# A graph, mixing and expert layer on one core: edge comparisons in five rounds, and work moved between waits

## The chip, the core and the metric

The kernel runs on one of the eight cores of a Trainium2 chip. A core has five engines with a program each: PE (TensorE, matrix products into PSUM, eight banks), DVE (VectorE), ACT (ScalarE), POOL (GpSimd) and SP (SyncE, which only starts transfers). They wait for one another by semaphores. The metric is the device time of one launch in microseconds, lower is better. Shown are three runs of the kernel before: 1836.55 us in the median, 1814.46 the lowest, 1837.39 the highest.

## The reference

x is 3125 x 256 with 53125 directed edges, sorted by destination. With n the layer norm of x:

```python
x = x + gnn(n, edges, ...) + mix(n, ...)      # both read the same n
x = x + ffn(layernorm(x), ...)
# gnn, three layers, widths 1024, 512, 256:
deg = segment_sum(1, dst) + 1; dinv = deg ** -0.5
h = relu(A @ (h @ W) + b), layer norm;  A[d, s] = edges(s, d) * dinv[s] * dinv[d], plus dinv^2 on the diagonal
# mix, on hyperbolic maps of n:
qkv = relu(batchnorm(n' @ Wqkv)); t = norm limits; s = pointwise(t)
out = (v k^T q) / (sum(v) + eps), per head;  ft = out @ Wres + b
```

The batch norm needs mean and variance of 768 columns over all rows. Edges may repeat, so the matrix A needs the number of equal (source, destination) pairs.

## The kernel before

The first third (0 to 350 us) does two things on the same engines. One is the mixing branch: rows of x are normed and turned, the Gram matrix of all rows is summed on PE, and the variance of each of the 768 columns comes from it: the matrix is turned and weighed with the weights (`weigh_gram_halves`), multiplied with the weights on DVE (`gw`), and summed by one-column matmuls (`bnsum_done`). Then five column blocks c of 625 rows each go through `hidden(c, m)` (six products of 12 matmuls into two pairs of banks, evacuated and squared by ACT), `spread(c, m)` (six products with `wp`), `norm_pair`, `norm_spread`, and on DVE `key`, `quotients`, `weigh`. Block c + 1's products stand in the program beside block c's quotients.

The other is the edges. Equal edges lie at most 40 places apart in the sorted list, or a flag says that they don't. DVE compares the key of each of 104 x 512 edges with those 1 to 40 places on (`equality`, `alike`, the result f16), and PE adds the 40 comparisons forwards and backwards into banks 6 and 7 by products with the identity (`count_alike`, 80 matmuls of 512 columns). The sums become an index and a value for each edge; PE turns them (`turn_edges`), DVE and ACT copy them out (`eidx`, `evalue`, L1737), and POOL scatters them into the matrix of counts in memory: 26 groups of 16 indirect transfers (L722). After the sixteenth transfer of a group it waits for the group before and raises `landed` (`landing`, L712 to L716). SP fetches one tile of counts for each row tile of the first layer, four buffers ahead at most, and waits for as many groups as that tile needs (L560). Degrees are counted by PE from one-hots (`degree(b)`, 16 matmuls) which DVE makes (`half_batch(b)`, L903 and L905, three buffers); there are 26 batches, of which `EARLY` come before the second block's products.

ACT also sums squares of the later weights (`weight_squares`, L1671, 28 pieces): pieces 0 to 12 stood between the veps of block 0 and the products of block 1.

From 350 us on, three layers of the graph network and the expert layer are bound by PE; the change doesn't touch them. Every order here is written out by hand.

## Time and profile before

| | us |
|---|---|
| median of three runs | 1836.55 |
| lowest, highest | 1814.46, 1837.39 |
| span of the profiled execution | 1299.6 |
| PE, DVE, POOL, ACT busy | 1189.9, 734.1, 563.5, 477.4 |

The profiler took one execution; the page gives its span from the first to the last instruction, and no other time of it. What lies around the span (launch and end) is the difference to a run's time, 537 us against the median. PE is busy for 92% of the span, but its share is lower in the first third, and a busy PE may run at half clock, so the row PEclk is read with it. A row of the trace in order of time gives start, duration, engine, line, operation, what it writes and reads, how many were merged, and in brackets how long the engine was idle before it and what ended that.

### The profile page before, as it was taken

To read this page: it belongs to the slowest core of one execution; us is meant where nothing else is said; L and a number is where in the kernel's file an instruction comes from. 1 tells how busy PE (TensorE), PEld (TensorE's weight loads), DVE (VectorE), ACT (ScalarE), POOL (GpSimd) and SP (SyncE) were. 2 spreads that over 40 slices of the span, in tenths; PEclk is the share of its full clock that TensorE was granted. 3 is DMA by queue.
4 is the path that set the end of the run, shared out by engine and by line. 5 is a ranking of instruction groups with operands and counts; after the bars stand their busy time and mean duration, and the time that the engine had idled before them with its cause. 6 is when DMAs were issued, how large, how long until landed. Compare 5 with 4: busy or idle time off the path is not lost.

```text
span 1299.6 us, 19205 instructions
## 1 busy us (share of the span) xinstructions
PE 1189.9 (92%) x6591; PEld 785.5 (60%) x6591; DVE 734.1 (56%) x1559; ACT 477.4 (37%) x1003; POOL 563.5 (43%) x579
## 2 busy tenths in 40 slices
PE   2897798988889999999999999999999899995995
PEld 2664465565556666666666566666666566652674
DVE  7875889687645554555455423333323388887253
ACT  4528565688432222222222113111111144441463
POOL 4207787778776777777774000350000000000633
PEclk9979989999889999999999999999999999998998
DMA  9881000001432222212143333323323256623201
GB/s 265 282 285 54 1 2 1 2 1 26 123 87 63 57 61 81 56 28 56 28 98 83 115 79 97 89 73 97 88 72 96 66 163 186 167 69 119 52 18 34
DMA packets 82936, 111.25 MB, mean 86 GB/s; under 512 B 51871, under 2 KB 67348, under 8 KB 82872
## 3 DMA queue, kind: packets, MB, share of 16 engines
q1 hardware_dynamic: 62344, 106.98, 29.9%
q0 software_dynamic: 20528, 3.47, 1.9%
q8 instruction: 34, 0.56, 0.2%
q14 instruction: 30, 0.25, 0.1%
HBM read 76.08 MB, written 27.67 MB: 80 GB/s over the span
## 4 chain that ended last, share of the span: by engine, by line
PE 83%; DVE 9%; ACT 5%; issue 2%; DMA 0%; POOL 0%; SPq 0%; ACTq 0%; DVEq 0%; POOLq 0%
PE psum L2044 80%; PE psum L2415 2%; DVE acc L903 1%; ACT acc L1613 1%; DVE scr L923 1%; ACT scr L1671 1%; DVE scr L1163 1%; PE psum L2408 0%; DVE scr L1469 0%; ACT scr L1741 0%; ACT scr L1767 0%; DVE big L917 0%; ACT scr L1748 0%; DVE acc L905 0%; DMA scr<-in_src_pad 0%
## 5 line engine op out<-in xcount | busy, mean ns | idle before, releaser
L722 POOL DMA_INDIRECT counts<-big,eidx x416 | 439.0, 1055 | 160.9 <-issue 160.9
L2044 PE MATMUL psum<-rows,scr 125*125 125x512 f16 x1250 | 276.4, 381 | 3.6 <-DVE rows L1266 1.6
L2044 PE MATMUL psum<-big,scr 125*125 125x512 f16 x1250 | 274.6, 379 | 1.0 <-DVE big L1300 1.0
L2044 PEld LDWEIGHTS psum<-rows,scr 125*125 125x125 f16 x1250 | 171.2, 137 | 104.1 <-issue 4.5
L2044 PEld LDWEIGHTS psum<-big,scr 125*125 125x125 f16 x1250 | 169.9, 137 | 96.5 <-DVE big L1300 1.5
L2044 PE MATMUL psum<-wb,scr 128*125 128x512 f16 x600 | 137.5, 379 | 1.4 <-DVE scr L1283 1.4
L2044 PEld LDWEIGHTS psum<-wb,scr 128*125 128x125 f16 x600 | 81.0, 136 | 45.9 <-DVE scr L1283 1.9
L774 POOL DMA_INDIRECT scr<-picked,eidx x13 | 22.9, 1758 | 182.7 <-issue 182.7
L1358 DVE SCALAR_TENSOR_TENSOR scr<-psum,col,wm 125x512 f32<-125x512 f32 x25 | 18.8, 751 | 128.9 <-PE psum L2044 128.9
L2044 PE MATMUL psum<-big,wm 128*128 128x313 f16 (+1 forms) x432 | 75.6, 328 | 8.8 <-ACT scr L1728 7.3
L1283 DVE TENSOR_TENSOR scr<-psum,scr 128x1000 f16<-128x1000 f32 x25 | 30.0, 1200 | 86.5 <-ACT scr L1882 86.5
L1940 ACT ACTIVATE scr<-scr 125x512 f32<-125x512 f32 x25 | 15.7, 629 | 166.1 <-DVE scr L1358 166.1
L828 DVE BATCH_NORM_STATS2 col<-scr 125x6 f32<-125x512 f32 x75 | 49.6, 689 | 45.5 <-ACT scr L1891 28.1
L2044 PE MATMUL psum<-wa,scr 128*125 128x512 f16 x300 | 71.8, 391 | 0.9 <-DVE scr L1278 0.9
L763 POOL IOTA scr<- 125x63 f32 x1 | 0.2, 201 | 159.9 <-PE psum L2044 159.9
L2044 PEld LDWEIGHTS psum<-big,wm 128*128 128x128 f16 (+1 forms) x432 | 48.1, 115 | 34.8 <-ACT scr L1728 8.1
L2044 PEld LDWEIGHTS psum<-wa,scr 128*125 128x125 f16 x300 | 42.3, 141 | 26.2 <-issue 2.6
L754 POOL TENSOR_SCALAR scr<-wa,col 128x512 f32<-128x512 f32 x4 | 6.4, 1591 | 116.4 <-DVE col L1374 116.1
L1882 ACT CAST scr<-psum 128x1000 f16<-128x1000 f32 x25 | 24.8, 992 | 81.2 <-PE psum L2044 71.8
L2044 PE MATMUL psum<-wm,scr 128*125 128x256 f32 (+2 forms) x156 | 41.7, 413 | 0.0
L2044 PE MATMUL psum<-acc 128*32 128x125 bf16 (+2 forms) x516 | 29.5, 257 | 12.8 <-DVE acc L905 11.4
L1163 DVE RECIPROCAL scr<-scr 128x626 f32<-128x626 f32 x10 | 40.7, 4066 | 0.3
(421 smaller groups left out, 1840.9 us busy)
## 6 DMA issues: line engine op xcount, KB each, us to landing
scr<-counts SPq DMA_DIRECT2D x75, 683.6 KB
counts<-wb SPq DMA_DIRECT2D x25, 683.6 KB
counts<-big,eidx POOLq DMA_INDIRECT x416
scr<-counts SPq DMA_DIRECT2D x75, 79.3 KB
scr<-in_x SPq DMA_DIRECT2D x25, 125.0 KB
picked<-big SPq DMA_DIRECT2D x5, 566.6 KB
rows<-in_x SPq DMA_DIRECT2D x5, 560.0 KB
out<-acc SPq DMA_DIRECT2D x5, 560.0 KB
```

Of the source, the lines that this page charges most:

```text
L722: pool.indirect_dma_start(cells, bass.IndirectOffsetOnAxis(ap=eidx[:, r * EQ + g:r * EQ + g + 1], axis=0), evalue[:, at_c:at_c + 1], None, ...
L774: pool.indirect_dma_start(got[:, g, :], None, picked_dram, bass.IndirectOffsetOnAxis(ap=picked[:, g:g + 1], axis=0), bounds_check=N - 1, o ...
L828: done.did(dve.bn_stats(st2[:, h, :], src[:, h * 512:(h + 1) * 512] if parts > 1 else src))
L903: done.did(dve.tensor_tensor(ohp, free(edp16, b * DB, [[2, DB // 2], [0, P], [1, 2]]), free(iop, 0, [[0, DB // 2], [2, P], [1, 2]]), ALU.i ...
L923: dve.tensor_tensor(alike[r % 2][:, lo:hi, :], free(ekey, 0, [[0, hi - lo], [1, EQW]]), free(ekey, 1 + r * SHIFTS + lo, [[1, hi - lo], [1, ...
L1163: done.did(dve.reciprocal(tdiv, tdiv))
L1283: dve.tensor_tensor(xT16[:, 1].rearrange("p (b k) q -> p b (k q)", b=2), turned_halves(), xT16[:, 0].rearrange("p (b k) q -> p b (k q)", b ...
L1358: dve.scalar_tensor_tensor(out=pre[b][:, 0:D2], in0=bank(b, P, D2), scalar=d2out[:, bass.ds(t, 1)], in1=b2r, op0=ALU.mult, op1=ALU.add).th ...
L1882: act.copy(xT16[:, 0].rearrange("p (b k) q -> p b (k q)", b=2), turned_halves()).then_inc(sem("xThi_done"), 1)
L1940: act.activation(pre[b][:, 0:D2], pre[b][:, 0:D2], ACT.Relu).then_inc(sem("relu2_done"), 1)
L2044: return pe.matmul(o, l, r, start=start, stop=stop)
L2415: last = pe.transpose(bank(5 + k // 4, 128, P, k % 4 * P), pre[0][:, k * 128:(k + 1) * 128], ident[:P, 0:P])
```

## The change

Nothing is computed otherwise. The edge comparisons come in five rounds of 8, 4, 10, 10 and 8 shifts, each with a place of its own where the memory is free (one in the region that the first products fill later), in place of four rounds of 10 in halves. Two rounds stand before the batch norm, one in its wait, two after it; the flag work comes behind the batch norm, and the flag's row is added on PE before the last two rounds are counted. The counts stand between the first block's products. Indices are turned after all six products. The flag is read by DVE behind round five. Five batches of one-hots and three of degrees move into the spread of block 0. ACT's squares 0 to 12 move behind the kept norms of block 1. POOL reports a group after four transfers of the next.

```diff
@@ -40,7 +40,7 @@
 DB = 16
-EARLY = 2
+EARLY = 5
 DEGREE_RUNS = (15, 11)
@@ -49,8 +49,8 @@
 HUGE = 3e38
-SHIFTS = 10
-ROUNDS_EQ = HALO // SHIFTS
+EQUAL_ROUNDS = ((0, 8), (8, 12), (12, 22), (22, 32), (32, 40))
+assert EQUAL_ROUNDS[-1][1] == HALO
 EQW = EC + HALO
@@ -254,8 +254,11 @@
-    alike = [scr[:ER, s * SHIFTS * EQW // 2:(s + 1) * SHIFTS * EQW // 2].bitcast(F16).rearrange(
-        "p (s i) -> p s i", s=SHIFTS) for s in range(2)]
+    ahead = big[:ER, pairs_at + 2 * 768:pairs_at + NT * CW]
+    behind = scr[:ER, at_edges + 7 * EW + 2 * EC:at_edges + 2 * NT * CW]
+    homes = (ahead, behind, scr[:ER, 0:5 * EQW], scr[:ER, 5 * EQW:10 * EQW], behind)
+    alike = [free(home.bitcast(F16), 0, [[EQW, hi - lo], [1, EQW]]) for home, (lo, hi) in zip(homes, EQUAL_ROUNDS)]
+    assert all((hi - lo) * EQW <= 2 * home.shape[1] for home, (lo, hi) in zip(homes, EQUAL_ROUNDS))
@@ -468,7 +471,7 @@
-    HALF_BATCHES = (((2, 2), (2, 2), (2, 5), (5, 8), (8, 12), (12, 15)),
+    HALF_BATCHES = (((5, 5), (5, 5), (5, 7), (7, 10), (10, 13), (13, 15)),
                     ((15, 16), (16, 16), (16, 18), (18, 22), (22, 24), (24, 26)))
@@ -722,8 +725,8 @@
                                             oob_is_err=False).then_inc(sem(f"scattered{n % 2}"), 16)
-            if n >= 1:
-                landing(n - 1)
+                if n >= 1 and r == n * ROWS_A_GROUP:
+                    landing(n - 1)
         landing(GROUPS - 1)
@@ -917,23 +920,21 @@
-        def equality(r, lo=0, hi=SHIFTS):
-            if r >= 2:
-                dve.wait_ge(sem("alike_used"), r - 1)
-            dve.tensor_tensor(alike[r % 2][:, lo:hi, :], free(ekey, 0, [[0, hi - lo], [1, EQW]]),
-                              free(ekey, 1 + r * SHIFTS + lo, [[1, hi - lo], [1, EQW]]), ALU.is_equal).then_inc(
-                sem("alike_ready"), hi - lo)
+        def equality(r):
+            lo, hi = EQUAL_ROUNDS[r]
+            if r == 4:
+                dve.wait_ge(sem("alike_used"), 2)
+            dve.tensor_tensor(alike[r], free(ekey, 0, [[0, hi - lo], [1, EQW]]),
+                              free(ekey, 1 + lo, [[1, hi - lo], [1, EQW]]), ALU.is_equal).then_inc(sem("alike_ready"), 1)
         done.settle()
         z_low(0)
         z_low(1)
-        equality(0, 0, 5)
+        equality(0)
         z_low(2)
-        equality(0, 5, 10)
         z_low(3)
-        equality(1, 0, 5)
         z_low(4)
-        equality(1, 5, 10)
+        equality(1)
         dve.wait_ge(milestone("zrow_done"), AFTER["zrow_done"])
@@ -959,6 +960,21 @@
                                      op0=ALU.mult, op1=ALU.subtract).then_inc(sem("wq_low"), 1)
+        dve.wait_ge(milestone("bnsum_done"), AFTER["bnsum_done"])
+        dve.tensor_scalar(tmp6, bank(3, 128, NT), 1.0 / N, None, ALU.mult).then_inc(milestone("bnvar_done"), 1)
+        done.did(dve.tensor_scalar(bnt, bank(3, 128, NT, 16), 1.0 / N, None, ALU.mult))
+        done.settle()
+        dve.wait_ge(milestone("bnroot_done"), AFTER["bnroot_done"])
...
+        dve.tensor_tensor(bnt, bnb, bnt, ALU.subtract).then_inc(milestone("bn_done"), 1)
+
         dstf = wkey
@@ -973,26 +989,12 @@
         done.did(dve.tensor_tensor(self_, free(dstf, HALO, [[1, EC]]), self_, ALU.is_equal))
-        dve.wait_ge(milestone("bnsum_done"), AFTER["bnsum_done"])
-        dve.tensor_scalar(tmp6, bank(3, 128, NT), 1.0 / N, None, ALU.mult).then_inc(milestone("bnvar_done"), 1)
-        done.did(dve.tensor_scalar(bnt, bank(3, 128, NT, 16), 1.0 / N, None, ALU.mult))
-        done.settle()
-        dve.wait_ge(milestone("bnroot_done"), AFTER["bnroot_done"])
...
-        dve.tensor_tensor(bnt, bnb, bnt, ALU.subtract).then_inc(milestone("bn_done"), 1)
-
         equality(3)
         dve.wait_ge(milestone("flag_part"), AFTER["flag_part"])
...
         done.settle()
+        equality(4)
         dve.wait_ge(milestone("flag_sum"), AFTER["flag_sum"])
@@ -1022,13 +1024,12 @@
-        dve.wait_ge(sem("alike_used"), ROUNDS_EQ)
+        dve.wait_ge(sem("alike_used"), len(EQUAL_ROUNDS))
         done.did(dve.tensor_tensor(bwd, bank(7, ER, EC), bwd, ALU.add))
-        done.did(dve.tensor_tensor(fwd, bank(6, ER, EC), fwd, ALU.add))
-        done.settle()
-
+        done.settle()
         done.did(dve.scalar_tensor_tensor(out=bwd, in0=bwd, scalar=2.0e7, in1=free(ekey, HALO, [[1, EC]]),
                                           op0=ALU.mult, op1=ALU.add))
+        done.did(dve.tensor_tensor(fwd, bank(6, ER, EC), fwd, ALU.add))
         done.settle()
@@ -1056,6 +1057,8 @@
         dve.tensor_scalar(needs[0:1, :], bank(6, 1, T, 128), 1.0, None, ALU.max).then_inc(milestone("needs_ready"), 1)
+        for b in range(2, EARLY):
+            half_batch(b)
         done.settle()
@@ -1732,9 +1735,6 @@
             hidden(0, m)
-            if m == 2:
-                act.wait_ge(milestone("value_turned"), AFTER["value_turned"])
-                act.copy(evalue, bank(7, 128, EQ * ER)).then_inc(milestone("value_kept"), 1)
@@ -1778,6 +1778,8 @@
+        act.wait_ge(milestone("value_turned"), AFTER["value_turned"])
+        act.copy(evalue, bank(7, 128, EQ * ER)).then_inc(milestone("value_kept"), 1)
         for m in range(NT):
@@ -1803,12 +1805,12 @@
                 rows_high(0, 4)
-            if c < 2:
+            if c == 1:
                 weight_squares(*SQUARES_AT[c][0])
             if c >= 1:
                 out_root(c - 1)
             besides(c, 0)
-            if c < 2:
+            if c == 1:
                 weight_squares(*SQUARES_AT[c][1])
@@ -1822,9 +1824,13 @@
             norm_keep(c + 1)
+            if c == 0:
+                weight_squares(*SQUARES_AT[c][0])
             veps_made(c + 1)
             out_square(c, 2)
             out_square(c, 3)
+            if c == 0:
+                weight_squares(*SQUARES_AT[c][1])
             besides(c, 3)
@@ -2047,14 +2053,16 @@
-        def count_alike(r, lo=0, hi=SHIFTS):
-            pe.wait_ge(sem("alike_ready"), r * SHIFTS + hi)
+        def count_alike(r, lo=0, hi=None):
+            first_shift, end = EQUAL_ROUNDS[r]
+            hi = end - first_shift if hi is None else hi
+            pe.wait_ge(sem("alike_ready"), r + 1)
             for k in range(lo, hi):
-                first, final = r + k == 0, r * SHIFTS + k == HALO - 1
-                behind = HALO - 1 - r * SHIFTS - k
-                mm(bank(6, ER, EC), ident16[:ER, 0:ER], alike[r % 2][:, k, HALO:HALO + EC], first, final)
-                last = mm(bank(7, ER, EC), ident16[:ER, 0:ER], alike[r % 2][:, k, behind:behind + EC], first, final)
-            if hi == SHIFTS:
+                shift = first_shift + k
+                after = HALO - 1 - shift
+                mm(bank(6, ER, EC), ident16[:ER, 0:ER], alike[r][:, k, HALO:HALO + EC], shift == 0, after == 0)
+                last = mm(bank(7, ER, EC), ident16[:ER, 0:ER], alike[r][:, k, after:after + EC], shift == 0, after == 0)
+            if hi == end - first_shift:
                 last.then_inc(sem("alike_used"), 1)
@@ -2126,7 +2134,7 @@
         last.then_inc(milestone("wq_summed"), 1)
-        count_alike(0, 3, SHIFTS)
+        count_alike(0, 3, 6)
@@ -2148,15 +2156,12 @@
         last.then_inc(milestone("wq_read"), 1)
-        count_alike(1, 0, 5)
+        count_alike(0, 6)
         pe.wait_ge(sem("wgw_done"), 1)
         for m in range(NT):
             last = mm(bank(3, 128, 1, m), gw[:, 0, m * 128:(m + 1) * 128], ones[:, 0:1], True, True)
         last.then_inc(milestone("bnsum_done"), 1)
-        count_alike(1, 5, SHIFTS)
-        pe.wait_ge(milestone("flag_part"), AFTER["flag_part"])
-        mm(bank(5, 1, 1, 400), ones[:ER, 0:1], flagf[:ER], True, True).then_inc(milestone("flag_sum"), 1)
-        count_alike(2)
+        count_alike(1)
@@ -2300,17 +2305,30 @@
-        for m in range(NT):
-            hidden(0, m)
-            if m == 0:
-                count_alike(3)
-            if m == 2:
-                turn_edges("index", 6, bwd)
-                turn_edges("value", 7, fwd)
+        hidden(0, 0)
+        count_alike(2, 0, 5)
+        hidden(0, 1)
+        count_alike(2, 5)
+        hidden(0, 2)
+        pe.wait_ge(milestone("flag_part"), AFTER["flag_part"])
+        mm(bank(5, 1, 1, 400), ones[:ER, 0:1], flagf[:ER], True, True).then_inc(milestone("flag_sum"), 1)
+        count_alike(3, 0, 5)
+        hidden(0, 3)
+        count_alike(3, 5)
+        count_alike(4)
+        hidden(0, 4)
+        hidden(0, 5)
+        turn_edges("index", 6, bwd)
+        turn_edges("value", 7, fwd)
+        spread(0, 0, 2)
         turn_reach()
-        spread(0, 0, 2)
+        spread(0, 2, 3)
         turn_needed()
-        spread(0, 2, NT)
+        degree(0)
+        spread(0, 3, 4)
+        degree(1)
+        spread(0, 4, NT)
+        degree(2)
         norm_pair(0, 5)
@@ -2324,7 +2342,7 @@
             if c == 0:
-                for b in range(EARLY):
+                for b in range(3, EARLY):
                     degree(b)
```

The milestones' names are put in the new order, and an assertion on sizes changes with them. The batch norm rows cut above are the same ones.

On PE, from the last counts before the Gram matrix is turned (`ident,scr 128x128`) up to the first product (`big,wm 128x313`, the next row before, and shown now); `scr,ident 104x512` and `big,ident 104x512` are counts. Before:

```order
L2044 MATMUL psum<-scr,ident 104x512 x14
L2134 MATMUL psum<-ident,scr 128x128
L2044 MATMUL psum<-wm,scr 128x512 x2
L2044 MATMUL psum<-wm,scr 128x256 x2
L2044 MATMUL psum<-wm,scr 128x512 x2
L2044 MATMUL psum<-wm,scr 128x256 x2
L2044 MATMUL psum<-col,wm 128x1 x12
L2044 MATMUL psum<-scr,ident 104x512 x10
L2044 MATMUL psum<-ones,big 128x1 x6
L2044 MATMUL psum<-scr,ident 104x512 x10
L2044 MATMUL psum<-col,ones 1x1
L2044 MATMUL psum<-scr,ident 104x512 x20
```

Now:

```order
L2050 MATMUL psum<-big,ident 104x512 x6
L2142 MATMUL psum<-ident,scr 128x128
L2050 MATMUL psum<-wm,scr 128x512 x2
L2050 MATMUL psum<-wm,scr 128x256 x2
L2050 MATMUL psum<-wm,scr 128x512 x2
L2050 MATMUL psum<-wm,scr 128x256 x2
L2050 MATMUL psum<-col,wm 128x1 x12
L2050 MATMUL psum<-big,ident 104x512 x4
L2050 MATMUL psum<-ones,big 128x1 x6
L2050 MATMUL psum<-scr,ident 104x512 x8
L2050 MATMUL psum<-big,wm 128x313 x12
L2050 MATMUL psum<-scr,ident 104x512 x10
```

Fewer counts stand before the turn and before the one-column products of the variance, and the first product comes after 12 + 12 of the 80 counts, not after 60.

On DVE, in the turning of the rows (L917, now L920, copies a turned block; L923, now L927, is `equality`) up to the correction of the Gram matrix (`col,psum 128x256`). Before:

```order
L923 TENSOR_TENSOR scr<-scr 104x2760
L917 SCALAR_TENSOR_TENSOR big<-psum,big 128x500 x2
L917 SCALAR_TENSOR_TENSOR big<-psum,big 128x2x125
L923 TENSOR_TENSOR scr<-scr 104x2760
L917 SCALAR_TENSOR_TENSOR big<-psum,big 128x500 x2
L917 SCALAR_TENSOR_TENSOR big<-psum,big 128x2x125
L923 TENSOR_TENSOR scr<-scr 104x2760
L917 SCALAR_TENSOR_TENSOR big<-psum,big 128x500 x2
L917 SCALAR_TENSOR_TENSOR big<-psum,big 128x2x125
L923 TENSOR_TENSOR scr<-scr 104x2760
L938 SCALAR_TENSOR_TENSOR scr<-big,col,psum 128x256
L940 SCALAR_TENSOR_TENSOR scr<-big,col,psum 128x128
```

Now:

```order
L927 TENSOR_TENSOR big<-scr 104x4416
L920 SCALAR_TENSOR_TENSOR big<-psum,big 128x500 x2
L920 SCALAR_TENSOR_TENSOR big<-psum,big 128x2x125
L920 SCALAR_TENSOR_TENSOR big<-psum,big 128x500 x2
L920 SCALAR_TENSOR_TENSOR big<-psum,big 128x2x125
L920 SCALAR_TENSOR_TENSOR big<-psum,big 128x500 x2
L920 SCALAR_TENSOR_TENSOR big<-psum,big 128x2x125
L927 TENSOR_TENSOR scr<-scr 104x2208
L939 SCALAR_TENSOR_TENSOR scr<-big,col,psum 128x256
L941 SCALAR_TENSOR_TENSOR scr<-big,col,psum 128x128
```

Four comparisons of five shifts have become one of eight and one of four.

On ACT, behind the kept norms (`acc<-psum 128x313`) of block 0 before, and of block 1 now; 1774 to 1778 is the veps root. Before:

```order
L1752 COPY acc<-psum 128x313
L1774 ACTIVATE scr<-psum,col 128x626
L1777 ACTIVATE scr<-scr,col 128x626
L1778 ACTIVATE acc<-psum,col 1x626
L1671 ACTIVATE scr,col<-wa 128x512 x4
```

Now:

```order
L1752 COPY acc<-psum 128x313
L1674 ACTIVATE scr,col<-wa 128x512 x4
L1674 ACTIVATE scr,col<-wb 128x512
L1674 ACTIVATE scr,col<-wb,col 128x512
L1674 ACTIVATE scr,col<-wb 128x512
L1674 ACTIVATE scr,col<-wb,col 128x512
L1774 ACTIVATE scr<-psum,col 128x626
```

Eight pieces of squares now stand ahead of block 1's veps root, and none behind block 0's.

## Rows read from the trace of the kernel before

**Rows 1.** Head of the page.

```profile
span 1299.6 us, 19205 instructions
```

**Rows 2.** DVE in time: start, duration, engine, line, operation, operands, count.

```profile
40.46 3.02 DVE L923 TENSOR_TENSOR scr<-scr 104x2760 f16<-104x2760 f32 x1
...
55.59 3.79 DVE L923 TENSOR_TENSOR scr<-scr 104x2760 f16<-104x2760 f32 x1
```

**Rows 3.** ACT in time; brackets give idle time before and what ended it.

```profile
53.15 0.37 ACT L1645 COPY big<-psum 128x256 f32<-128x256 f32 x1 [2.11 <-PE psum L2044]
```

**Rows 4.** PE in time, 51 to 105 us.

```profile
51.17 1.50 PE L2044 MATMUL psum<-scr,ident 104*104 104x512 f16 x6 [0.55 <-DVE big L917]
...
53.32 3.21 PE L2044 MATMUL psum<-scr,ident 104*104 104x512 f16 x14
...
60.08 0.33 PE L2134 MATMUL psum<-ident,scr 128*128 128x128 f32 x1 [3.56 <-DVE scr L940]
...
75.32 4.49 PE L2044 MATMUL psum<-scr,ident 104*104 104x512 f16 x10
...
86.48 1.78 PE L2044 MATMUL psum<-big,wm 128*128 128x313 f16 x12
...
102.86 2.30 PE L2044 MATMUL psum<-big,wm 128*128 128x313 f32 x8
```

**Rows 5.** Stretches: length; PE, PEld, DVE, ACT, POOL busy; PEclk, DMA, GB/s.

```profile
80.00:84.00 4.00, 4.00 (x10) 2.01 (x11) 4.00 (x1) 0.00 (x0) 0.00 (x0) 0.50 0.94 320
...
88.00:103.00 15.00, 15.00 (x108) 9.60 (x107) 6.22 (x13) 9.15 (x12) 3.20 (x3) 1.00 0.79 268
```

**Rows 6.** ACT in time, squares and veps root.

```profile
117.53 0.61 ACT L1671 ACTIVATE scr<-wa 128x512 f32<-128x512 f32 x1
...
160.19 0.78 ACT L1774 ACTIVATE scr<-psum,col 128x626 f32<-128x626 f32 x1 [7.32 <-DVE scr L1173]
```

**Rows 7.** PE in time, 116 to 134 us.

```profile
116.28 0.66 PE L2044 MATMUL psum<-acc 128*32 128x125 bf16 x32
...
127.72 5.60 PE L2044 MATMUL psum<-big,wm 128*128 128x313 f16 x24 [5.84 <-ACT scr L1728]
```

**Rows 8.** DVE in time, 116 to 170 us.

```profile
116.46 0.81 DVE L1173 TENSOR_TENSOR big<-psum,big 128x626 f32<-128x626 f32 x1 [10.31 <-PE psum L2044]
...
135.27 0.81 DVE L1173 TENSOR_TENSOR scr<-psum,scr 128x626 f32<-128x626 f32 x1 [1.74 <-PE psum L2044]
...
139.59 1.20 DVE L903 TENSOR_TENSOR acc<-acc,scr 128x2000 bf16<-128x2000 bf16 x1 [3.51 <-PE psum L2044]
...
142.55 1.19 DVE L903 TENSOR_TENSOR acc<-acc,scr 128x2000 bf16<-128x2000 bf16 x1
...
169.21 0.81 DVE L1173 TENSOR_TENSOR scr<-psum,scr 128x626 f32<-128x626 f32 x1 [0.64 <-PE psum L2044]
```

**Rows 9.** PE in time, last two tiles of layer 1.

```profile
678.36 5.56 PE L2044 MATMUL psum<-rows,scr 125*125 125x512 f16 x25
...
692.60 5.56 PE L2044 MATMUL psum<-rows,scr 125*125 125x512 f16 x25
```

**Rows 10.** POOL in time, scatters and the last landing.

```profile
98.93 1.24 POOL L722 DMA_INDIRECT counts<-big,eidx  x1 [30.27 <-issue]
...
652.05 0.97 POOL L722 DMA_INDIRECT counts<-big,eidx  x1 [0.30 <-issue]
...
670.20 1.08 POOL L722 DMA_INDIRECT counts<-big,eidx  x1 [0.30 <-issue]
...
672.44 0.10 POOL L716 MEMSET col<- 125x1 f32 x1 [1.04 <-DMA counts<-big,eidx]
```

**Rows 11.** SyncE's queue in time, the fetch of tile 23.

```profile
671.58 0.86 SPq L513 DMA_DIRECT2D scr<-counts  x2
```

**Rows 12.** Stretches of 1 us around an undisturbed fetch, columns as in rows 5.

```profile
514.00:515.00 1.00, 1.00 (x6) 0.64 (x5) 0.68 (x2) 0.00 (x0) 0.69 (x2) 1.00 0.10 13
...
519.00:520.00 1.00, 1.00 (x7) 0.60 (x6) 0.00 (x0) 0.62 (x1) 0.80 (x1) 1.00 0.13 32
```

More of the change, by code:

```diff
@@ L93 @@
     "zscale_ready1", "gram_copied",
-    "wqscale_done", "flag_part", "bnvar_done", "bn_done", "flag_ready", "index_ready", "value_ready", "edges_ready", "reach_ready", "needed_ready",
+    "wqscale_done", "bnvar_done", "bn_done", "flag_part", "flag_ready", "index_ready", "value_ready", "edges_ready", "reach_ready", "needed_ready",
     "needs_ready", "squares_summed", "dinv_read", "scales_ready", "be2w_read", "n4_ready", "f4_ready", "be3w_read", "fscale_done",
@@ L229, in _build @@
     wq_high = scr[:, at["scr"] - 882:at["scr"] - 882 + 768].bitcast(F16).rearrange("p (k n) -> p k n", k=2)
-    assert at["scr"] - 882 == SHIFTS * EQW
+    assert at["scr"] - 882 >= 10 * EQW
     gram = take("scr", 512).rearrange("p (k n) -> p k n", k=2)
@@ L961, in _ @@
                                      op0=ALU.mult, op1=ALU.subtract).then_inc(sem("wq_low"), 1)
+        dve.wait_ge(milestone("bnsum_done"), AFTER["bnsum_done"])
[3 more added lines that the diff above has]
+        dve.wait_ge(milestone("bnroot_done"), AFTER["bnroot_done"])
+        done.did(dve.reciprocal(tmp6, tmp6))
+        done.settle()
+        done.did(dve.tensor_tensor(bns, tmp6, bng, ALU.mult))
+        done.settle()
+        done.did(dve.tensor_tensor(bnt, bnt, bns, ALU.mult))
+        done.settle()
+        done.did(dve.tensor_scalar(bns, bns, wq_back, 1.0 / Z_SCALE, ALU.mult, ALU.mult))
+        done.settle()
+        dve.tensor_tensor(bnt, bnb, bnt, ALU.subtract).then_inc(milestone("bn_done"), 1)
         dstf = wkey
@@ L975, in _ @@
         done.did(dve.tensor_tensor(self_, free(dstf, HALO, [[1, EC]]), self_, ALU.is_equal))
-        dve.wait_ge(milestone("bnsum_done"), AFTER["bnsum_done"])
-        dve.tensor_scalar(tmp6, bank(3, 128, NT), 1.0 / N, None, ALU.mult).then_inc(milestone("bnvar_done"), 1)
-        done.did(dve.tensor_scalar(bnt, bank(3, 128, NT, 16), 1.0 / N, None, ALU.mult))
-        done.settle()
-        dve.wait_ge(milestone("bnroot_done"), AFTER["bnroot_done"])
-        done.did(dve.reciprocal(tmp6, tmp6))
-        done.settle()
-        done.did(dve.tensor_tensor(bns, tmp6, bng, ALU.mult))
-        done.settle()
-        done.did(dve.tensor_tensor(bnt, bnt, bns, ALU.mult))
-        done.settle()
-        done.did(dve.tensor_scalar(bns, bns, wq_back, 1.0 / Z_SCALE, ALU.mult, ALU.mult))
-        done.settle()
-        dve.tensor_tensor(bnt, bnb, bnt, ALU.subtract).then_inc(milestone("bn_done"), 1)
         equality(3)
```

## The prediction

> **What bounds the kernel now.** I read the page first. The span is 1299.6 us [rows 1], and nearly all of the chain that ended last is PE's; what it does not have on PE lies mostly in the first third, so the question is which waits end last there. The busy digits show where the engines meet, and I then read each engine in order of time.
>
> From 40 to 60 us DVE is the late one. It fits a piece of edge comparisons (2760 elements, 3.02 us at 40.46) behind each copy of turned rows, the last one from 55.59 to 59.3, and only then corrects the Gram matrix [rows 2]. ACT had the operand of that correction at 53.15 + 0.37 = 53.5 [rows 3]. PE waits 3.56 us and turns the matrix at 60.08. From there to 102.86, where the first product of the second kind starts, PE is never idle, but works at half clock for part of it: ten counting matmuls take 4.49 us at 75.32 against 3.21 us for fourteen at 53.32, 449 against 229 ns each [rows 4]. The granted clock says the same: 0.50 in 80 to 84, 1.00 in 88 to 103 [rows 5]; the first is 1.2 GHz, and it follows the gap and a run of one-column matmuls.
>
> From 116 to 169 us two things alternate. ACT squares weights from 117.53 until one evacuation before 127.72, 9.2 us for twelve, 0.77 each [rows 6], and the evacuation of the next products stands behind them: PE waits 5.84 us and restarts at half clock, 24 matmuls in 5.60 us [rows 7]. DVE waits for PE's sums at 135.27 and for a free one-hot buffer at 139.59, 1.74 and 3.51 us. Then it makes one-hots at (142.55 - 139.59) / 2 = 1.48 us a batch and PE waits for it, until the keys of the second column block are read at 169.21 [rows 8].
>
> Layer 1 is PE without gaps: the last two tiles start at 678.36 and 692.60, 14.24 us apart [rows 9]. Beside it GpSimd scatters edge counts from 98.93 to 672.44 [rows 10], and the fetch of a counts tile waits for the groups it needs. That race is nearly lost already: the fetch of the last tile but one (tile 23) is issued at 671.58 [rows 11]. A fetch is in flight about 4.9 us, by an undisturbed one whose traffic starts in 514 to 515 and is down to 0.13 of the engines in 519 to 520 [rows 12]. So 678.36 - 671.58 - 4.9 = 1.9 us is all the slack of tile 23.
>
> **The change, part by part.**
> Comparisons. Before the correction DVE now compares 12 shifts instead of 20: 8 in one instruction (4416 elements at 1.09 ns, 4.8 us, ending 45.3, some 0.2 us after the next copy could begin) and 4 behind the last copy (2.4 us). Three copies stand between, 4.7 us by the gaps between the pieces, so DVE is free at 52.4. ACT's operand then decides, about 53.0, since PE's first six counting matmuls no longer wait 0.55 us [rows 4]. PE's six further ones end at 54.2, and the matrix is turned there: **5.9 us earlier** than 60.08. Of the 14 counting matmuls that stood ahead of it, 8 have moved behind it: minus 8 x 0.229 = 1.8 us. PE then has four counting matmuls where it had ten beside DVE's 10-shift comparison (6.0 us by the same rate) and the making of the variance operand; up to 6 x 0.229 = 1.4 us may open, I take 0.9: minus 0.9. Batch norm comes ahead of the flag work on DVE; with eight counting matmuls beside it I get the first product at about 70 instead of 86.48. The other 56 stand between the products; they are the same work, only later in order. The flag's sum and its read are waited for by SyncE's branch and weight load, which is used 50 us later. Round five waits until round two is counted, long past; behind it on DVE stands only that flag read. So nothing new ends last, provided round three (flag work, then 6.0 us) ends near 79, before PE wants it near 82.
> Clock. Of the stretch from 60 to 103 some 17 us ran at 1.2 GHz, a cost of 8.5 us. The 3.56 us gap goes, the one-column matmuls stay. I take 10 us at half, a cost of 5.1: **3.4 us gained**. No row shows the new interleave; its ends are 8.5 gained (never half) and 18 lost (half throughout, rival B). I stay near the rows of the stretch itself [rows 5], less the gap's share.
> Spread of block 0. Three degree batches move in, 0.33 us each by the two at 116.28 [rows 7], and with them minus 1.1. DVE builds their one-hots in its waits. Sum to the keys of block 0 (116.46 [rows 8]): 5.9 - 1.8 - 0.9 + 3.4 - 1.1 = **5.5 us**.
> One-hots and squares, 116 to 169. Three fewer batches on DVE: 3 x 1.48 = 4.4 us. The waits of 1.74 and 3.51 go, because ACT's squares no longer hold PE and because five batches, not two, are used early, so the buffers are free; that of 0.64 at 169.21 may go too. I set 0.5 us against it for the last batch. 4.4 + 5.9 - 0.5 = **9.8 us**; if the waits come back whole it is 4.4. The squares (eight of them 6.1 us) now stand between the kept norms and the veps root of block 1, where ACT sat 7.32 us idle until 160.19 [rows 6]; DVE reads that root only behind the keys of block 1, so some 3 us more are hidden. The other four, 3.1 us, lie ahead of a copy that PE's sums release later. Without that cover they cost the whole 9.2 us.
> Scatter. ACT's copy of the values stands behind three more products, and turning the indices behind as many on PE, but all comes earlier: I get 98.6 us for the first scatter against 98.93. SyncE's queue is passed by nothing. The hoisted landing is reported after 4 scatters of the next group instead of 16: 12 x 1.27 = 15.2 us sooner for all tiles but the last. GpSimd would stall if a scatter took longer than four issues, 5.1 us; the last is issued at 670.20 and its landing ends a wait at 672.44 [rows 10], 2.2 us, so no stall. I cost it at nothing, and it keeps the rest: PE will want tile 23 at 678.36 - 15.3 = 663.1, and its fetch may go at about 656. For the last tile the final landing still rules: 672.1 + 0.4 + 4.9 = 677.4 against 692.60 - 15.3 = 677.3.
> **Sum:** 5.5 + 9.8 = 15.3, less 0.1 to 0.5 for the last tile: 15 us, span 1284.6. Later stages are untouched. The page gives the profiled run no time beside its span; against the median of the runs shown, 1836.55, 537 us lie around it, and I keep them: **1821.5 us**. Against the lowest run, 1814.46, it would be 1799.5.
>
> **A rule weighed.** After the wait of 5.84 us PE runs at half clock [rows 7], and in 80 to 84 it is at 0.50 though never idle [rows 5]: dense work after sparse work did not raise it at once. The Trainium skill, "TensorE: Matmul & The Clock Gate", section "A second HAM failure mode: psum-queue depth-cycling", says that small idles between groups of matmuls can make the clock swing between its two levels; by that the finer interleave speaks against the change, and the time would be rival B's. The trace agrees only in part: 88 to 103 alternates products and counts already, at 1.00.
>
> **Rivals.**
> A. The scatter race eats it. If the landing is not reported sooner in effect (GpSimd stalls at each group), tile 23 stays at 671.6 + 4.9 = 676.5 and PE can gain only 1.9 us: 1834.7. For it: the race is at its limit. Against: 2.2 us a scatter. With scatters 5 us late in all it is 10 us gained, 1826.5. Chance 0.15 together.
> B. Slower than before: the clock stays at 1.2 GHz through the interleave. Six products of 1.78 us and 56 counting matmuls of 0.229, 23.5 us, take 47 where my sum has 25.5: 21.5 lost, 15 gained, **1843**. It decides from the point where over two thirds of that stretch is at half. Against: no wait over 1 us is left there. Chance 0.04.
> C. DVE's chain from 116 on gives half, its waits returning a batch later: 10 us gained, 1826.5. Chance 0.2.
> D. Round three comes late to PE and the comparisons give 4 us less: 1825.5. Chance 0.1.
> Forecast: 0.51.
>
> **The numbers.** All cases but B lie between 1821 and 1835 on the median. The runs shown spread 23 us with one program, one of three low; a median that falls low would be 1799.5. The range takes that in and ends above rival A, 1799 to 1837; outside lie B and a rest, together under 0.2. Two per cent is 37 us, about what a measurement of this kernel can tell from no change; no case reaches it by itself, only a low median comes close: faster 0.05, same 0.92, slower 0.03.
>
> **What would show it.** PE turns the Gram matrix near 54; the first product starts near 70, the first spread near 97; the clock in 75 to 97 is 1.00. ACT has no squares between the first veps and the next products, and PE's gap of 5.84 us is gone. The keys of block 1 are read near 154. Tile 23's fetch is issued near 656, the last near 672.6, and PE has no gap at 677. I am wrong if the landing memsets lie much over 21 us apart late in the scatter, if PE waits for comparisons after 78, or if layer 1 starts later than 341.

## The result, and the profile after

| runs side by side | before, median | changed, median | ratio, 95% interval |
|---|---|---|---|
| first chip (the result) | 1833.55 us | 1818.74 us (1799.34 to 1821.67) | 0.9892 [0.9853, 0.9931] |
| chip 15 | 1836.47 us | 1830.10 us | 0.9954 [0.9937, 0.9972] |
| chip 13 | 1301.99 us | 1289.41 us | 0.9902 [0.9881, 0.9922] |

The forecast was 1821.5 us, and 15 us of gain; measured were 14.8 us. The number is right, but one statement under it is false, and part of the agreement is luck. The time of a run is its span plus 1.86 us (1819.06 against 1817.2), so no 537 us lie around a span. They lie in it: both kernels have been seen in two conditions, near 1300 and near 1830 us, which no edit here chose; each set of runs was in one of them throughout, and near 1830 us the kernel before also has a few runs near 1798 and 1817 beside its 1836. The profile shown of before was taken in the other condition than the times shown.

The page of the changed kernel, from the result's own run (PE, PEclk and POOL: 40 slices of 45 us, in tenths):

```profile
span 1817.2 us, 19203 instructions
...
PE   4971201010001119887899999999999999999796
...
POOL 3177777666666660000100000021023000000143
...
PEclk9895555555555559999999999999999999999898
```

Before layer 1 there is a stretch of some 570 us, from 112 us to a little behind GpSimd's last scatter, in which PE is nearly empty and at half clock. It is called the hole from here on, and a run without it undisturbed. In time (start, duration, engine, line, operation, operands, count, idle before) PE and GpSimd look like this in it, and at its end:

```profile
322.46 0.26 PE L2050 MATMUL psum<-acc 128*32 128x125 bf16 x1 [2.54 <-issue]
325.26 0.26 PE L2050 MATMUL psum<-acc 128*32 128x125 bf16 x1 [2.54 <-issue]
...
322.39 0.97 POOL L725 DMA_INDIRECT counts<-big,eidx  x1 [0.30 <-issue]
323.66 0.97 POOL L725 DMA_INDIRECT counts<-big,eidx  x1 [0.30 <-issue]
...
501.89 0.97 POOL L725 DMA_INDIRECT counts<-big,eidx  x1 [0.43 <-issue]
503.30 0.97 POOL L725 DMA_INDIRECT counts<-big,eidx  x1 [0.44 <-issue]
...
681.15 0.97 POOL L725 DMA_INDIRECT counts<-big,eidx  x1 [0.30 <-issue]
...
685.48 2.45 PE L2050 MATMUL psum<-scr,kones 128*128 128x313 f32 x4
687.86 1.48 PE L2050 MATMUL psum<-big,ones 128*32 128x375 f32 x8
```

A matmul every 2.80 us, waiting for nothing that the profile names, beside scatters 1.27 to 1.40 us apart (1.41 in the mean over all 416). That is about one matmul for two scatters, but not in step: beside the same 2.80 us the scatters are 1.28 us apart at 322 us. ACT and DVE stand still for up to 148 us at a time, much of it put down to "another core or an unknown queue", and then run a group of instructions at their usual pace (ACT starts a square each 0.76 us from 565.0 to 571.2 us, as in the undisturbed run from 138.5 on). Nearly all block work is still to do when the last scatter ends: 1817.2 - 681.2 = 1136 us, where the undisturbed run shown next has 1289.5 - 112 = 1177.5 us left when the hole would begin. 570 us did the work of 41.

The undisturbed condition, chip 13, is the one that answers to the rows ahead of the prediction. The page and PE in time there:

```profile
span 1289.5 us, 19203 instructions
...
PE   2998799887999999999999999999999899996995
```

```profile
53.40 0.27 PE L2142 MATMUL psum<-ident,scr 128*128 128x128 f32 x1
...
69.00 2.38 PE L2050 MATMUL psum<-big,wm 128*128 128x313 f16 x12
71.22 2.32 PE L2050 MATMUL psum<-scr,ident 104*104 104x512 f16 x10
73.38 1.78 PE L2050 MATMUL psum<-big,wm 128*128 128x313 f16 x12
...
337.72 5.56 PE L2050 MATMUL psum<-rows,scr 125*125 125x512 f16 x25
...
662.51 5.61 PE L2050 MATMUL psum<-rows,scr 125*125 125x512 f16 x25 [0.72 <-DMA scr<-counts]
...
679.86 7.30 PE L2050 MATMUL psum<-rows,scr 125*125 125x512 f16 x25 [2.90 <-DMA scr<-counts]
```

DVE in time in the same run:

```profile
39.95 4.75 DVE L927 TENSOR_TENSOR big<-scr 104x4416 f16<-104x4416 f32 x1
...
108.39 0.81 DVE L1176 TENSOR_TENSOR big<-psum,big 128x626 f32<-128x626 f32 x1 [4.84 <-PE psum L2050]
...
151.32 0.81 DVE L1176 TENSOR_TENSOR scr<-psum,scr 128x626 f32<-128x626 f32 x1 [0.64 <-PE psum L2050]
```

And the forecast stretch (PE, PEld, DVE, ACT, POOL busy; then PEclk):

```profile
75.00:97.00 22.00, 22.00 (x140) 13.01 (x137) 14.93 (x19) 10.12 (x15) 1.26 (x1) 1.00 0.86 297
```

Against [rows 4, 8]: the Gram matrix is turned at 53.40 (forecast 54, before 60.08), the first product starts at 69.0 (70), the clock in 75 to 97 is 1.00 (1.00; before it was 0.50 in part of it [rows 5]), the keys of block 0 are read at 108.4 (111), of block 1 at 151.3 (154). The first layer-1 work, 25 matmuls, starts at 337.7, 15.7 us before the 353.43 of the kernel before run again on that chip. Then PE waits for counts where it never did, and at layer 2 only 11.3 of the 15.7 are left (720.26 against 731.60).

### The profile page after: what moved, and what is told of

Its sections match the earlier page's. It is cut to its first block, busy times and chain, and to the rows that moved or that the text cites. A ratio compares the mean times of both kernels' runs of the same rounds, so it can differ in the third digit from the quotient of the medians.

```text
span 1817.2 us, 19203 instructions
## 1 busy us (share of the span) xinstructions
PE 1232.1 (68%) x6591; PEld 794.8 (44%) x6591; DVE 733.1 (40%) x1558; ACT 478.1 (26%) x1003; POOL 540.9 (30%) x579
## 4 chain that ended last, share of the span: by engine, by line
PE 59%; issue 19%; another core or an unknown queue 12%; DVE 5%; ACT 4%; DMA 1%; POOL 0%; SPq 0%; ACTq 0%; DVEq 0%; POOLq 0%
PE psum L2050 57%; PE psum L2433 1%; ACT big L1724 0%; ACT scr L1741 0%; ACT acc L1616 0%; DMA scr<-picked,eidx 0%; ACT scr L1731 0%; PE psum L2426 0%; ACT scr L1767 0%; DVE big L927 0%; DVE scr L927 0%; ACT scr L1748 0%; DVE scr L1472 0%; DVE scr L1166 0%
## 5 line engine op out<-in xcount | busy, mean ns | idle before, releaser
L725 POOL DMA_INDIRECT counts<-big,eidx x416 | 416.3, 1001 | 200.5 <-issue 164.2
L906 DVE TENSOR_TENSOR acc<-acc,scr 128x2000 bf16<-128x2000 bf16 x26 | 31.1, 1194 | 506.4 <-remote 377.6
L2050 PE MATMUL psum<-acc 128*32 128x125 bf16 (+2 forms) x516 | 53.8, 263 | 223.0 <-issue 218.2
L2050 PEld LDWEIGHTS psum<-acc 128*32 128x32 bf16 (+1 forms) x516 | 32.1, 121 | 244.6 <-issue 237.4
L2050 PE MATMUL psum<-scr,wm 128*128 128x313 f32 x48 | 22.9, 574 | 144.2 <-ACT scr L1741 110.6
L1741 ACT ACTIVATE scr<-psum 128x626 f32<-128x626 f32 x30 | 20.9, 695 | 367.2 <-remote 186.6
L750 POOL TENSOR_TENSOR acc<-acc,wm 125x256 f32<-125x256 f32 x25 | 17.1, 729 | 333.6 <-DVE acc L1292 333.6
L2050 PE MATMUL psum<-big,ones 128*32 128x313 f32 (+1 forms) x204 | 34.0, 515 | 77.9 <-issue 66.6
L2050 PEld LDWEIGHTS psum<-scr,wm 128*128 128x128 f32 x48 | 11.3, 244 | 158.4 <-ACT scr L1741 114.3
```

What stands on the lines that cost most here:

```text
L725: pool.indirect_dma_start(cells, bass.IndirectOffsetOnAxis(ap=eidx[:, r * EQ + g:r * EQ + g + 1], axis=0), evalue[:, at_c:at_c + 1], None, ...
L750: pool.tensor_tensor(accv[:, t, :], accv[:, t, :], be3r, ALU.add).then_inc(sem("be3_added"), 1)
L906: done.did(dve.tensor_tensor(ohp, free(edp16, b * DB, [[2, DB // 2], [0, P], [1, 2]]), free(iop, 0, [[0, DB // 2], [2, P], [1, 2]]), ALU.i ...
L1741: act.activation(halves(sTs[c % 2][:, m, :]), pair(m % 2), ACT.Relu if m < 4 else ACT.Copy).then_inc(sem("s_evac"), 1)
L2050: return pe.matmul(o, l, r, start=start, stop=stop)
```

## The experiments

Theory R is the record's: a gain ahead of layer 1, kept because the landing is reported sooner. Theory F came with the hole: the time is the end of the scatters plus what is left then. Four sets of runs, 12 in all. F can be tried only where the hole is.

**The kernel before, again** (a0_before_again).

> The kernel before, once more, to have its trace beside the one after. Theory F (stretch theory): from about 112 us to the last scatter every engine issues about one instruction per scatter, as the trace after shows; then this run's span is near 1833 us and not 1299.6, its scatters end some 1 to 2 us later than 683 us, and what is left to do then takes about 1148 us against 1134. Rival (the record's own): the 537 us lie around the span, which is again near 1300 us.

1301.82 us against 1300.64 in the same set, 0.9993 [0.9972, 1.0014]; span 1300.4, no hole. This chip is in the other condition, so its set speaks on R and not on F. That the span is 1300 was the rival's forecast, but the run's time is 1302.22, not 1837: nothing lies around it.

**The landing back in its old place** (e_land16).

```
-                if n >= 1 and r == n * ROWS_A_GROUP:
-                    landing(n - 1)
+            if n >= 1:
+                landing(n - 1)
```

> The change, but a group's landing is reported behind the sixteenth scatter of the next group again, as in the kernel before. Theory F: no fetch of counts stands at the end of a scatter in layer 1, so the hoist is worth nothing: the same as the change, about 1819 us. Rival (the record's own): tile 23 comes 15 us later for PE, which keeps 1.9 us of its gain: about 1832 us.

1298.31 us, 0.9990 [0.9972, 1.0007]: 2.3 us faster than before, not clear of noise, where R kept 1.9. The gain is gone. PE's waits (waited for; us in total, times, longest), of this kernel and then of the change:

```profile
PE psum L2050 <- DMA scr<-counts: 12.3, 3, 6.7
```

```profile
PE psum L2050 <- DMA scr<-counts: 3.6, 2, 2.9
```

Layer 1 starts at 335.46, 2.3 us sooner than in the change, yet layer 2 at 729.05 instead of 720.26. R is right in this condition: without the sooner report PE waits 12.3 us for counts, with it 3.6, and from layer 1 to layer 2 it takes 393.6 us instead of 382.5.

**Four groups of 26, and 13** (e_few, e_half).

```
+        KEPT = 4        # 13 in e_half
...
+                    if n < KEPT:
                         pool.indirect_dma_start(cells, ...)
```

> The change, but only the first 4 of the 26 groups are scattered; the edge counts of the other 22 are left out. Theory F: the slow stretch ends with the scatters, near 97 + 4 x 22 = 185 us, and the span is about 1290 to 1310 us. Rival, that 537 us lie around the span whatever the scatters do: time stays near 1819 us.

> The change with only the first 13 of the 26 groups scattered; the edge counts of the other 13 are left out. In the condition of 1835 us, Theory F: the slow stretch ends with the scatters near 97 + 208 x 1.40 = 388 us instead of 680, and the time falls by about 290 us to about 1535 us. In the condition of 1300 us, record: as with 4 groups, the race is gone and nothing else, 1285 to 1286.5 us. Rival for either: the scatters' number is nothing to the slow stretch, about 1820 us.

1286.53 us (0.9891 [0.9860, 0.9923]) and 1284.46 us (0.9869 [0.9836, 0.9903]). Both met the undisturbed condition, so they don't test whether fewer scatters end the hole. They do show what the race still costs the change: with 13 groups layer 1 starts at 337.78 as in the change and layer 2 at 712.95, 375.2 us later instead of 382.5 (with 4 groups at 340.00 and also 375.2 us later). Of the 7.3 us, 3.6 are the two waits, 7.30 - 5.61 = 1.7 the lower clock behind the second. The last 1.65 are half clock in the first tile. They are not the race's, for w_sooner below has all its scatters and not this stretch. Twelve matmuls there, in e_half and then in the change:

```profile
345.77 2.80 PE L2054 MATMUL psum<-wa,scr 128*125 128x512 f16 x12 [0.91 <-DVE scr L1285]
```

```profile
345.70 4.45 PE L2050 MATMUL psum<-wa,scr 128*125 128x512 f16 x12 [0.91 <-DVE scr L1281]
```

**GpSimd slowed on purpose** (e_paced): ahead of each scatter

```
+                    for _ in range(4):
+                        done.did(pool.memset(paced[:, :], 0.0))
+                        done.settle()
```

> The change, with four small chained memsets on GpSimd (an estimate: 0.5 us together) between any two scatters, 416 scatters in all. Theory F1, that the rate at which GpSimd hands out scatters saturates what the engines' issue shares: the stretch dissolves and the time falls below 1450 us. Theory F2, that each scatter outstanding costs the others an issue, whatever the pace: the stretch grows to about 416 x 1.8 = 750 us and the time is about 1870 us. The record's own theory, that the engines are not held by scatters: tiles of layer 1 wait for the later landings and the time rises by less than 60 us.

1738.75 us, 1.3368 [1.3325, 1.3411]; undisturbed condition, so F1 and F2 stay untried. All forecasts missed, R's too, since the memsets cost twice my estimate: the scatters run from 96.9 to 1117.7 us, 2.46 us each instead of 1.39. 415 x 1.07 = 445 us later, and the time rises by 438 against before, 449 against the change. PE waits 406 us for counts:

```profile
L2054 PE MATMUL psum<-rows,scr 125*125 125x512 f16 x1250 | 318.0, 420 | 409.6 <-DMA scr<-counts 405.9
```

So once the scatters are slower than in the change, their pace bounds the kernel nearly one for one.

**The change again** (a1_after_again, a2_after_again).

> The change itself, once more, beside kernels whose engines did not slow down during the scatter. The record's theory (race, gain ahead of layer 1): 15 us less than before in the same runs, near 1285.5 us against 1300.6, with the Gram matrix turned near 54, the keys of block 1 read near 154, tile 23's fetch near 656 and no wait of PE at 677. Theory F (the gain of the first pair of medians came from work done before and during the slow stretch, and without that stretch there is none): 1300 us.

> The change itself. Two conditions of the chip have been seen with the kernel before: about 1300 us (engines at their own pace beside the scatters) and about 1835 us (every engine issues about one instruction per scatter). Record's theory: in the first condition 15 us less than before, near 1285.5 us, keys of block 1 read near 154, tile 23's fetch near 656, no wait of PE at 677. Theory F: without the slow stretch there is no gain, 1300 us. In the second condition both say little: 5 to 15 us less than before.

The first met the hole: 1830.10 us, 6.4 less than before. The second did not: 1289.41 us, 12.6 less (10 to 15.5 by its interval). F's forecast of no gain without the hole falls, R's holds to 3.9 us; the waits for counts and the clock behind them are 5.4. Tile 23's fetch went at 657.38 (forecast 656), the last at 674.10 (672.6), and the gap at 677, which the record excluded, is there.

**The parts** (p_onlyland, p_both and the same kernel again as b1_both, p_oldsq). p_onlyland is before with only the landing moved. p_both takes two parts back out of the change:

```
-EARLY = 5
+EARLY = 2
...
-            if c == 1:
+            if c < 2:
                 weight_squares(*SQUARES_AT[c][0])
```

with the old table of batches and the third degree batch out of the spread of block 0; p_oldsq takes back the squares alone.

> The kernel before with the sooner landing report alone. Record: before had 1.9 us of slack at tile 23, so nothing to gain: 1300.6 us, within 1 us; tile 23's fetch at about 656 all the same. Rival (fetches of counts hold PE already in the kernel before, or a GpSimd queue held by each group's landing is what sets the pace of the scatters): 3 us or more faster.

> The change with the squares of block 0's weights back between the products and two early one-hot batches instead of five: the five rounds of comparisons, the batch norm's place and the landing alone. Record: the 5.5 us up to the keys of block 0 less the 1.1 of three degree batches that stay later, and the old waits behind: 1296 us. Rival, that the two parts behind the comparisons did nothing, because DVE's chain takes the place of the waits: as the change, 1286.

> The change with the squares of block 0's weights back between the products (behind the first veps root, ahead of the evacuations of block 1). Record: the waits of 1.74 and 3.51 us that come from the late start of the products come back in part, and PE's gap of 5.84 us is there again: 3 to 5.5 us slower than the change, about 1290 us. Rival (with five batches made early, DVE has its own work while PE is late): within 1 us of the change.

> The comparisons in five rounds, the batch norm's place and the sooner landing alone; squares and one-hots as in the kernel before. Record: in the condition of 1300 us it keeps 4.4 us of the 15, 1296 us (5.5 less the 1.1 of the degree batches). Rival, that this part alone brings all: 1286 us. In the condition of 1835 us: within 5 us of before, as seen once.

| kernel | condition | median us | ratio to before | last scatter starts | rest of span |
|---|---|---|---|---|---|
| p_onlyland | hole | 1836.19 | 0.9979 [0.9947, 1.0011] | 677.6 | 1158.4 |
| p_both | hole | 1834.18 | 1.0124 [1.0074, 1.0174] | 674.7 | 1156.9 |
| p_oldsq | hole | 1823.51 | 0.9934 [0.9917, 0.9951] | 673.2 | 1147.1 |
| change (a1) | hole | 1830.10 | see above | 678.3 | 1149.6 |
| change (result) | hole | 1818.74 | see above | 681.1 | 1136.1 |
| b1_both | undisturbed | 1292.36 | 0.9930 [0.9904, 0.9956] | 665.8 | 624.7 |

(The ratio of p_both says little: its median is 2.3 us under that of before, 1836.47.) The span is the sum of the two last columns whatever the theory; what F adds is that no edit moves the end of the scatters. It moves by 8 us, and not as the edits would have it.

But the last scatter does not end the hole. In p_oldsq PE goes on by single matmuls for ten us behind it:

```profile
673.22 0.97 POOL L725 DMA_INDIRECT counts<-big,eidx  x1 [0.30 <-issue]
675.35 0.10 POOL L719 MEMSET col<- 125x1 f32 x1 [1.16 <-DMA counts<-big,eidx]
```

```profile
681.28 0.26 PE L2046 MATMUL psum<-acc 128*32 128x125 bf16 x1 [1.83 <-issue]
683.38 0.26 PE L2046 MATMUL psum<-acc 128*32 128x125 bf16 x1 [1.84 <-issue]
684.11 0.61 PE L2046 MATMUL psum<-acc 128*32 128x125 bf16 x15 [0.46 <-issue]
```

In the five traces with the hole the engines are back at 685.2 (the result), 684.0 (a1), 683.1 (p_onlyland), 680.8 (p_both) and 684.1 (p_oldsq), 4.1 to 10.9 us behind the last scatter, and in p_both and p_oldsq, whose scatters end first, it is longest. So what F rests on, that the hole ends with the scatters, the rows don't bear out.

Counted from the last scatter as in the table, the rest is 1157 to 1158 us without the squares' and one-hots' new places, and 1136 to 1150 with them or the one-hots' alone. One profile of each; what within that is noise I can't say, and the change itself shows both 1136 and 1150. p_oldsq was forecast 3 to 5.5 us slower than the change, by the rival within 1 us; beside a1 it was 6.6 us faster, so neither came. It met the hole, and no undisturbed run has the squares alone, so they stay untried. So does the landing alone: p_onlyland, within 1 us of before as forecast, met the hole too.

b1_both was forecast at 1296 and gave 1292.4. Its layer 1 starts at 347.79, 5.6 us sooner than before (forecast 4.4 to 5.5), and the other two parts bring the next 10.1 us (337.72; forecast 9.8). These are single traces: the change, e_land16, e_half and e_few, which differ only in what GpSimd does, start layer 1 at 335.46 to 340.00, so an agreement within 1 us is partly luck. But from layer 1 to layer 2 it takes 375.2 us where before took 378.2 and the change 382.5. Before ran the work from 361 to 380 partly at 1.2 GHz (12 matmuls 4.37 us there, 2.80 here), a stretch that I had not read. And b1_both has no wait for counts, since its last scatter starts at 665.8, the change's at 671.7. That is why the two are 3 us apart and not 10.

**Scatters sooner** (w_sooner), to beat both: the last counts ahead of products 3 and 4, the turning ahead of product 5.

```
-        hidden(0, 3)
         count_alike(3, 5)
         count_alike(4)
+        hidden(0, 3)
         hidden(0, 4)
-        hidden(0, 5)
         turn_edges("index", 6, bwd)
         turn_edges("value", 7, fwd)
+        hidden(0, 5)
```

(and ACT's copy of the values behind its fifth evacuation).

> The change, and the rest of the counting matmuls ahead of products 3 and 4 of block 0, index and values turned ahead of product 5: the first scatter about 2.7 us sooner (near 93 us instead of 95.7). In the condition of 1300 us, race theory (what the change lost is the last groups' lateness: PE waited 0.72 and 2.90 us for counts and then ran 25 matmuls at half clock, 1.7 us): the waits shrink to about 0.9 us, 3 to 4.5 us faster than the change, a ratio to before near 0.987. Rival (the scatters' start does not set their end, since GpSimd is held by something else): as the change, ratio 0.990. In the condition of 1835 us: at most 3 us less than the change.

1288.59 us, 0.9899 [0.9875, 0.9924]: no different from the change. The first scatter did not come sooner: 96.40 us, where the eight traces with the change's order up to there have 95.4 to 97.0. PE's counts ended at 88.7, but DVE did not read them; in time:

```profile
84.94 0.14 DVE L999 TENSOR_SCALAR col<-psum 1x1 f32<-1x1 f32 x1
85.11 0.14 DVE L1001 CAST col<-col 1x1 int32<-1x1 f32 x1
91.09 0.69 DVE L1028 TENSOR_TENSOR scr<-psum,scr 104x512 f32<-104x512 f32 x1 [5.84 <-issue]
```

Between the two the program has only the load of the flag into a register, the branch on it, and a wait for counts that were done. The waits for counts stayed, 0.95 and 2.19 us. Here the scatters are released by the flag, not by the counts. What of the 5.84 us is the load, and what the branch, no run separates.

## Why the prediction was right, and where not

**Comparisons, batch norm, clock: right.** Each mark came within 3 us. Forecast to the keys of block 0: 5.5 us less; measured 115.18 - 108.39 = 6.8. The clock's means in 60 to 70, 70 to 80 and 80 to 90 us are 0.67, 0.99 and 1.00, and 0.88, 0.50 and 0.93 in before on that chip: some 7 us less at half clock, worth 3.5 us, an estimate from these means (forecast 3.4). Rival B is out (1.00 in 75 to 97), and so is D: PE has no gap there. The rule that I weighed, of the Trainium skill, "TensorE: Matmul & The Clock Gate", section "A second HAM failure mode: psum-queue depth-cycling", spoke for B. It speaks of small idles between groups of matmuls; this trace has none from 65.6 to 104.0 us, so it does not test the rule, and what I had wrong is that the interleave would bring them.

**Flag: costed at nothing, and wrong.** I said that its read is used 50 us later. DVE itself branches on it: from the cast to DVE's next instruction stand 5.2 to 6.5 us in each undisturbed trace. In w_sooner the counts were done 2.4 us before, so there the 5.84 us are the flag's; in the change both end together (counts at 89.39, DVE at 89.43).

**One-hots and squares: right in sum, not taken apart.** 9.8 us forecast, 10.1 measured at layer 1 from b1_both to the change. At the keys of block 1 the gain over before is 166.79 - 151.32 = 15.5, so between the two keys it was 15.5 - 6.8 = 8.7: this term came 1.1 short and the one ahead of it 1.3 over. That their sum, 15.5, met the 15.3 of the forecast so closely is partly luck. ACT has no squares ahead of the evacuations of block 1 and PE's gap of 5.84 is gone; b1_both still has it.

**The landing: right in kind, and needed.** Its forecast was 13.4 us kept (15.3 against 1.9); taking it back costs 8.8 us at layer 2, 11.1 us from layer 1 to layer 2. It is no gain of its own but decides how much of the others is kept. "So no stall" did not hold throughout. Once GpSimd waited for the last scatters of a group, in the change:

```profile
319.04 0.10 POOL L719 MEMSET col<- 125x1 f32 x1 [1.35 <-DMA counts<-big,eidx]
```

e_land16 and b1_both have no such wait before their last landing.

**The last tiles: the term that failed.** "Less 0.1 to 0.5 us for the last tile" came to 3.6 us of waits and 1.7 of clock. PE was ready for the last tile at 676.96, as forecast (677.3); the counts came at 679.86 instead of 677.4. Of these 2.5 us 1.6 are the later last landing and its fetch, issued at 674.10 instead of 672.5, and 0.9 the fetch itself, 5.76 us instead of 4.9. The 1.7 us of clock are not the price of any such wait: behind 2.19 us in w_sooner and 3.54 in e_land16 the same 25 matmuls took 5.61 us.

I had the scatters end where they ended before. They started 1.1 us sooner than in before on the same chip (95.74, 96.85) and ended 1.1 later (671.68, 670.54). The way there was not even: the change was 2.7 us behind at the 26th scatter (137.06, 134.34), 4.8 at the 33rd, level at the 251st (455.55, 455.58), and behind again at the end. e_land16, as slow at first (137.55), ended 2.1 us sooner, at 669.55. So the loss at the start doesn't by itself explain the end; the wait of 1.35 us above is part of it, and the rest stays open. Against b1_both, which differs only in one-hots and squares, the loss is early and stays: 1.0 us ahead at the first scatter, 4.6 behind at the 26th, 5.8 at the last (665.84). GpSimd beside DVE in the change:

```profile
100.59 1.18 DVE L906 TENSOR_TENSOR acc<-acc,scr 128x2000 bf16<-128x2000 bf16 x1
...
102.04 1.18 DVE L906 TENSOR_TENSOR acc<-acc,scr 128x2000 bf16<-128x2000 bf16 x1
...
112.97 4.07 DVE L1166 RECIPROCAL scr<-scr 128x626 f32<-128x626 f32 x1
```

```profile
100.06 4.34 POOL L725 DMA_INDIRECT counts<-big,eidx  x1 [0.30 <-issue]
...
114.09 0.97 POOL L725 DMA_INDIRECT counts<-big,eidx  x1 [0.30 <-issue]
...
121.32 1.78 POOL L725 DMA_INDIRECT counts<-big,eidx  x1 [0.30 <-issue]
123.40 1.14 POOL L725 DMA_INDIRECT counts<-big,eidx  x1 [0.30 <-issue]
124.85 1.85 POOL L725 DMA_INDIRECT counts<-big,eidx  x1 [0.31 <-issue]
```

A scatter takes 0.97 us beside the reciprocal (one operand). From 95 to 340 us 96 of the change's scatters overlap a DVE instruction that reads two operands from SBUF, and take 1.32 us in the mean, up to 4.38; the other 80 all take 0.97. By 135.8 us the change has issued 25 scatters, before 27. In 95 to 160 DVE is busy 57.7 us in the change, 48.5 in b1_both and 45.2 in before. So the waits taken from DVE were gaps in which GpSimd ran at full pace. It fits the hole, where DVE mostly stands still: up to 340 us 171 of 192 scatters there overlap no such instruction, and none of the 171 takes over 0.98. No run tried it alone. The Trainium skill, "SBUF — State Buffer", section "SBUF: two separate sides", has a rule of this kind: the pair of ports that GpSimd shares with VectorE is held for a whole instruction, by a VectorE instruction in a 2-port mode, or by one with two SBUF inputs against a GpSimd instruction that reads SBUF. The trace agrees as to what stands beside the long scatters, with these durations; which of the two cases it is, no row shows. I did not weigh it.

**537 us "around the span": false.** They are the hole. No trace of the kernel before has the hole. In p_onlyland, the nearest to it, 1158.4 us are left behind the last scatter, in the change 1136.1 and 1149.6; so with the hole the gain seems to be work done ahead of its end, which is argued and not shown. That it was about the same 15 us is luck and no confirmation of the steps: between 6.4 and 14.8 us were measured there, on two chips. What brings the hole is open. It is not one kernel's: on chip 15 both have it by their times, on chip 13 neither. Nor is it the landing, which stands in its old place in one of them and in its new place in the other. The pages with the hole put 12 to 28% of the chain to "another core or an unknown queue", the undisturbed ones none: that something outside this program holds the engines is a rival that no run tried. It is not shown either that the scatters bring it or end it: it outlasts them by 4.1 to 10.9 us, and pacing or fewer scatters could not be tried in it.

## What to carry to other kernels

Compare each run's time with the profile's own span before anything is summed: here 537 us between them were another condition, and the time around the span was 1.86 us. Where a second engine races the bound one, a gain counts only up to the race's slack, and the slack must be worked out from how the race's pace changes with the edit: here scatters were longer beside VectorE's two-operand instructions, so VectorE's idle time was worth something to GpSimd. Before moving the counts that a branch waits for, look whether the branch's own flag comes later.

## What was not expected of the hardware

- In one condition PE issues a matmul each 2.80 us at PEclk 0.50 and ACT and DVE stand for up to 148 us between groups of instructions, for some 570 us. The scatters run in that time, but it outlasts the last of them by 4 to 11 us. The expectations above say "every engine issues about one instruction per scatter". For ACT and DVE the rows don't bear that out, and for PE only roughly: 31 matmuls and 30 weight loads beside 77 scatters in 150 to 250 us. The same program on another chip runs at full pace beside the scatters.
- A scatter of one element a partition: 0.97 us alone, up to 4.38 beside VectorE's two-operand work; four chained memsets of 128x8 between scatters cost 1.07 us, not 0.5.
- A flag read into a register and branched on: 5.84 us between two DVE instructions in w_sooner, 6.50 in before run again.
